# A four-layer cross-attention kernel: its long products issued as four products of 32 output rows, and its value products in blocks of two steps in place of four

## The reference

```python
q = (xn @ wq.T).reshape(B, S, NUM_HEADS, HEAD_DIM)       # x: (8, 100, 128)
k = (kvn @ wk.T).reshape(B, K, NUM_HEADS, HEAD_DIM)      # ctx: (8, 1444, 128)
v = (kvn @ wv.T).reshape(B, K, NUM_HEADS, HEAD_DIM)
scores = jnp.einsum('bshd,bkhd->bhsk', q, k) * scale
attn = jax.nn.softmax(scores, axis=-1)
o = jnp.einsum('bhsk,bkhd->bshd', attn, v).reshape(B, S, D_MODEL)
...
x = _L0_xattn_ref(x, ctx_1024, ...)
x = _L1_xattn_ref(x, ctx_1024, ctx_1024, mask_Bx1xSxS2_bf0, ...)
x = _L2_xattn_ref(x, ctx_1024, ...)      # ff = gelu(att_h @ W1.T + b1) @ W2.T + b2
x = _L3_xattn_ref(x, ctx_1024, ctx_1024, ...)
```

## Time and profile before

| | before |
|---|---|
| median of 3 runs | 1116.84 us (1113.83 to 1118.72) |
| the profiled execution | 1119.34 us, of which the span of its instructions is 1117.6 us |
| PE busy | 1000.5 us, 90% of the span, 9658 products and as many weight loads |
| DVE busy | 818.8 us, 73% |
| ACT busy | 762.0 us, 68% |
| mean granted clock of PE | 0.96 of 2.4 GHz |

### The profile page before, as it was taken

One profiled execution on the slowest core, in us unless ns is written; L12 is line 12 of the kernel. 1 busy time (PEld: TensorE's weight loads), 2 busy tenths in 40 slices (PEclk: granted clock), 3 DMA queues, 4 the chain that ended last, 5 costly groups with the idle time before them and its releaser, 6 DMA issues.

```text
span 1117.6 us, 25480 instructions
## 1 busy us (share of the span) xinstructions
PE 1000.5 (90%) x9658; PEld 554.8 (50%) x9658; DVE 818.8 (73%) x1687; ACT 762.0 (68%) x1692; POOL 414.7 (37%) x411
## 2 busy tenths in 40 slices
PE   0579999999989999999998999999999999998996
PEld 0235555555545555555454555555555545454442
DVE  5697787788767778887887776767677777676851
ACT  1157777876768787878777666666666675757675
POOL 5865545545412341334124142424333342423100
PEclk9979999999999999999999898989898989899999
DMA  8232212321222232223222120202020212111100
GB/s 211 67 94 81 75 52 64 81 72 50 82 63 68 82 105 66 79 81 102 70 81 79 30 80 19 81 18 81 18 83 19 82 36 65 45 55 54 31 4 5
DMA packets 64449, 72.98 MB, mean 65 GB/s; under 512 B 8210, under 2 KB 59994, under 8 KB 64198
## 3 DMA queue, kind: packets, MB, share of 16 engines
q1 hardware_dynamic: 64326, 71.33, 22.7%
HBM read 50.35 MB, written 18.15 MB: 61 GB/s over the span
## 4 chain that ended last, share of the span: by engine, by line
PE 62%; DVE 21%; ACT 8%; issue 5%; POOL 2%; SPq 1%; DMA 0%; POOLq 0%; ACTq 0%; DVEq 0%
PE acc L733 16%; PE ring L674 15%; PE sexp L713 14%; DVE mx L1105 6%; DVE mneg L1111 4%; DVE mx L1103 3%; PE ring L607 3%; PE ring L619 3%; ACT probs L981 2%; PE ring L797 2%; ACT kp L927 2%; PE ring L648 2%; DVE max L1206 1%; SPq L462 1%; ACT sc L1006 1%
## 5 line engine op out<-in xcount | busy, mean ns | idle before, releaser
L1105 DVE TENSOR_TENSOR mx<-ring,mx 120x400 f16<-120x400 f32 (+1 forms) x1056 | 554.5, 567 | 197.0 <-PE ring L674 194.7
L981 ACT ACTIVATE probs<-sexp 120x400 f32<-120x400 f32 (+1 forms) x1152 | 539.6, 513 | 197.5 <-PE sexp L713 192.6
L674 PE MATMUL ring<-qx,krep 96*128 96x400 f16 (+2 forms) x1152 | 398.7, 351 | 43.0 <-ACT kp L927 14.6
L713 PE MATMUL sexp<-qx,krep 97*128 97x400 f16 (+2 forms) x1152 | 396.3, 348 | 8.8 <-ACT probs L981 5.0
L733 PE MATMUL acc<-probs,vx 120*18 120x200 f32 (+1 forms) x4608 | 258.7, 343 | 0.8 <-ACT probs L981 0.7
L713 PEld LDWEIGHTS sexp<-qx,krep 97*128 97x128 f16 (+2 forms) x1152 | 127.0, 111 | 141.1 <-ACT probs L981 79.7
L674 PEld LDWEIGHTS ring<-qx,krep 96*128 96x128 f16 (+2 forms) x1152 | 127.7, 111 | 128.1 <-DVE mx L1105 30.9
L733 PEld LDWEIGHTS acc<-probs,vx 120*18 120x18 f32 (+1 forms) x4608 | 108.0, 98 | 115.7 <-issue 81.8
L481 POOL TENSOR_TENSOR kp<-kf,kp 128x480 f16<-128x480 f32 (+1 forms) x72 | 79.4, 1108 | 204.6 <-ACT kp L927 204.6
L519 POOL TENSOR_TENSOR qx<-qs,headmask 96x400 f16<-96x400 f16 x96 | 80.1, 864 | 54.1 <-PE sexp L713 30.3
L498 POOL TENSOR_TENSOR rstd<-vare,half 100x1 f32<-100x1 f32 x24 | 13.0, 543 | 214.3 <-DVE vare L1122 214.3
(11 more groups left out here) (131 smaller groups left out, 906.4 us busy)
## 6 DMA issues: line engine op xcount, KB each, us to landing
krep<-kept SPq DMA_DIRECT2D x144, 120.0 KB, 2.6
ctf<-in_ctxT SPq DMA_DIRECT2D x16, 722.0 KB
kept<-kp SPq DMA_DIRECT2D x48, 240.0 KB, 2.7
krep<-kept SPq DMA_DIRECT2D x72, 121.0 KB, 3.0
kept<-kp SPq DMA_DIRECT2D x24, 242.0 KB, 2.5
nat<-in_ctx SPq DMA_DIRECT2D x8, 720.0 KB
maskexp<-maskmax SPq DMA_DIRECT2D x8, 281.2 KB, 3.4
anymask<-in_mask SPq DMA_DIRECT2D x1, 1128.1 KB, 7.2
```

What stands on the lines that cost most here:

```text
L674: last = pe.matmul(ps[0:n, 0:QW], krep[0:PARTS, u.par, t, c0:c0 + n], qx[0:PARTS, u.third, t, :, :].rearrange("p f s -> p (f s)"), start=T ...
L713: last = pe.matmul(ps[0:n, 0:QW], krep[:, u.par, t, c0:c0 + n], qx[:, u.third, t, :, :].rearrange("p f s -> p (f s)"), start=True, stop=no ...
L981: act.activation(probs[0:r, j % PR, :], sexp[j % SR][0:r, 0:QW], ACT.Exp).then_inc(sem["probs_ready"], 1)
L1105: op = dve.tensor_tensor(dst, src, dst, ALU.max)
```

## The change

A helper `grouped` issues a product as up to four products of at most 32 output rows each: rows 0 to 31, 32 to 63, 64 to 95 and 96 to the end, each with its own weight load of at most 32 columns. All products of more than 32 output rows go through it except the values' projection (L619), the products of 9 columns (L797), and the transposes of the context, of the mask and of the maxima (L596, L629, L689), which stay as they were. Transposes that go through it (L637, L744, L750, L761, L787, L805) are no longer issued as transposes but as products with the identity; in float32 PE runs each of those as two instructions where it ran one. The number of blocks of values doubles and each has half the products.

```diff
-TOGETHER = 4
+TOGETHER = 2
 VALUES_AT = [j // TOGETHER * TOGETHER + TOGETHER + SR - 1 for j in range(NSTEP)]
...
+        def grouped(run, out, w, x, **flags):
+
+            for g in range(0, out.shape[0], 32):
+                m = min(32, out.shape[0] - g)
+                last = run(out[g:g + m], w[:, g:g + m], x, **flags)
+            return last
...
                 for j, (w, c) in enumerate(((0, 0), (0, 1), (1, 0))):
-                    last = pe.matmul(ps[:, 0:n], wk16[:, w, u.L, :], ct[:, u.par, c, c0:c0 + n], start=(j == 0),
-                                     stop=(j == 2))
+                    last = grouped(pe.matmul, ps[:, 0:n], wk16[:, w, u.L, :], ct[:, u.par, c, c0:c0 + n], start=(j == 0),
+                                   stop=(j == 2), skip_group_check=True)
...
-                last = pe.matmul(ps[0:n, 0:QW], krep[0:PARTS, u.par, t, c0:c0 + n],
-                                 qx[0:PARTS, u.third, t, :, :].rearrange("p f s -> p (f s)"),
-                                 start=True, stop=not masks, skip_group_check=masks)
+                last = grouped(pe.matmul, ps[0:n, 0:QW], krep[0:PARTS, u.par, t, c0:c0 + n],
+                               qx[0:PARTS, u.third, t, :, :].rearrange("p f s -> p (f s)"),
+                               start=True, stop=not masks, skip_group_check=masks)
...
                 for t in range(T):
-                    last = pe.transpose(ps[0:S, 128 * t:128 * t + 128], osb[:, S * t:S * t + S], ident[:, :])
+                    last = grouped(pe.matmul, ps[0:S, 128 * t:128 * t + 128], osb[:, S * t:S * t + S], ident[:, :], start=True,
+                                   stop=True)
...
                 for h in range(HT):
-                    last = pe.transpose(ps[0:S, S * h:S * h + S], sc2[:, HT * t + h, :], ident[0:S, 0:S])
+                    last = grouped(pe.matmul, ps[0:S, S * h:S * h + S], sc2[:, HT * t + h, :], ident[0:S, 0:S], start=True,
+                                   stop=True)
```

More of the change, by code:

```diff
@@ L636, in inputs @@
                 ps = begin("xT", u)
-                pe.transpose(ps[:, 0:S], xcur[:, :], ident[0:S, 0:S]).then_inc(sem["xT_filled"], 1)
+                grouped(pe.matmul, ps[:, 0:S], xcur[:, :], ident[0:S, 0:S], start=True, stop=True).then_inc(sem["xT_filled"], 1)
             def queries(u):
@@ L645, in queries @@
                 if u.L:
-                    pe.matmul(ps[0:PARTS, 0:T * S], bq16[:, u.L, :], which16[:, :], start=True, stop=False, skip_group_check=True)
+                    grouped(pe.matmul, ps[0:PARTS, 0:T * S], bq16[:, u.L, :], which16[:, :], start=True, stop=False,
+                            skip_group_check=True)
                 for t in range(T):
-                    last = pe.matmul(ps[0:PARTS, S * t:S * t + S], wq[:, u.L, t, :], xT[:, :], start=not u.L, stop=True,
-                                     skip_group_check=u.L > 0)
+                    last = grouped(pe.matmul, ps[0:PARTS, S * t:S * t + S], wq[:, u.L, t, :], xT[:, :], start=not u.L,
+                                   stop=True, skip_group_check=u.L > 0)
                 last.then_inc(sem["q_filled"], 1)
             def add_mask(ps, tile, which, c, r):
-                return pe.matmul(ps.rearrange("p (h s) -> p h s", h=HT), masked_by[0:r, which, 0:r],
-                                 tile[0:r, c, :].unsqueeze(1).broadcast_to([r, HT, S]), start=False, stop=True,
-                                 skip_group_check=True)
+                return grouped(pe.matmul, ps.rearrange("p (h s) -> p h s", h=HT), masked_by[0:r, which, 0:r],
+                               tile[0:r, c, :].unsqueeze(1).broadcast_to([r, HT, S]), start=False, stop=True,
+                               skip_group_check=True)
             def columns(c):
@@ L712, in exp_product @@
                 n = columns(c)
-                last = pe.matmul(ps[0:n, 0:QW], krep[:, u.par, t, c0:c0 + n],
-                                 qx[:, u.third, t, :, :].rearrange("p f s -> p (f s)"),
-                                 start=True, stop=not masks, skip_group_check=masks)
+                last = grouped(pe.matmul, ps[0:n, 0:QW], krep[:, u.par, t, c0:c0 + n],
+                               qx[:, u.third, t, :, :].rearrange("p f s -> p (f s)"),
+                               start=True, stop=not masks, skip_group_check=masks)
                 if masks:
@@ L749, in output_back @@
                 ps = begin("OT", u)
-                pe.transpose(ps[:, 0:S], oatt[:, 0, :], ident[0:S, 0:S]).then_inc(sem["oT_filled"], 1)
+                grouped(pe.matmul, ps[:, 0:S], oatt[:, 0, :], ident[0:S, 0:S], start=True, stop=True).then_inc(sem["oT_filled"], 1)
             def project(u):
@@ L754, in project @@
                 ps = begin("wo", u)
-                pe.matmul(ps[0:S, 0:D], oT[:, :], wo[:, u.L, :], start=True, stop=True).then_inc(sem["wo_filled"], 1)
+                grouped(pe.matmul, ps[0:S, 0:D], oT[:, :], wo[:, u.L, :], start=True, stop=True).then_inc(sem["wo_filled"], 1)
             def context_input2(u):
@@ L760, in context_input2 @@
                 ps = begin("cx2", u)
-                pe.transpose(ps[:, 0:S], x2[:, :], ident[0:S, 0:S]).then_inc(sem["cx2_filled"], 1)
+                grouped(pe.matmul, ps[:, 0:S], x2[:, :], ident[0:S, 0:S], start=True, stop=True).then_inc(sem["cx2_filled"], 1)
             def keys_queries_values2(u):
@@ L766, in keys_queries_values2 @@
                 ps = begin("kqv2", u)
-                pe.matmul(ps[:, 0:S], wk[:, 2, :], cx2[:, 0, :], start=True, stop=True)
+                grouped(pe.matmul, ps[:, 0:S], wk[:, 2, :], cx2[:, 0, :], start=True, stop=True)
                 for t in range(T):
                     pe.matmul(ps[32 * t:32 * t + 32, S:2 * S], wq[:, 2, t, 0:32], cx2[:, 1, :], start=True, stop=True)
-                pe.matmul(ps[0:S, 2 * S:2 * S + D], cx2[:, 0, :], wv[:, 2, :], start=True, stop=True
-                          ).then_inc(sem["kqv2_filled"], 1)
+                grouped(pe.matmul, ps[0:S, 2 * S:2 * S + D], cx2[:, 0, :], wv[:, 2, :], start=True, stop=True
+                        ).then_inc(sem["kqv2_filled"], 1)
             def scores2(u, t):
@@ L777, in scores2 @@
                 ps = begin(f"s2{t}", u)
-                pe.matmul(ps[0:S, 0:QW], q2[:, :], kbd2[:, HT * t:HT * t + HT, :].rearrange("p h s -> p (h s)"),
-                          start=True, stop=True).then_inc(sem["s2_filled"], 1)
+                grouped(pe.matmul, ps[0:S, 0:QW], q2[:, :], kbd2[:, HT * t:HT * t + HT, :].rearrange("p h s -> p (h s)"),
+                        start=True, stop=True).then_inc(sem["s2_filled"], 1)
             def transposed2(u, t):
@@ L804, in attention_back2 @@
                 ps = begin("at2", u)
-                pe.transpose(ps[:, 0:S], att2[:, :], ident[0:S, 0:S]).then_inc(sem["at2_filled"], 1)
+                grouped(pe.matmul, ps[:, 0:S], att2[:, :], ident[0:S, 0:S], start=True, stop=True).then_inc(sem["at2_filled"], 1)
             def hidden2(u):
@@ L810, in hidden2 @@
                 for j in range(FF // 128):
-                    last = pe.matmul(ps[:, S * j:S * j + S], w1[:, 128 * j:128 * j + 128], aT2[:, :], start=True, stop=True)
+                    last = grouped(pe.matmul, ps[:, S * j:S * j + S], w1[:, 128 * j:128 * j + 128], aT2[:, :], start=True,
+                                   stop=True)
                 last.then_inc(sem["h2_filled"], 1)
@@ L817, in feed_forward2 @@
                 for j in range(FF // 128):
-                    last = pe.matmul(ps[0:S, 0:D], hT[:, j, :], w2[:, j, :], start=(j == 0), stop=(j == FF // 128 - 1))
+                    last = grouped(pe.matmul, ps[0:S, 0:D], hT[:, j, :], w2[:, j, :], start=(j == 0), stop=(j == FF // 128 - 1),
+                                   skip_group_check=True)
                 last.then_inc(sem["w2_filled"], 1)
```

## The result

The changed kernel takes 1122.8 us (median of 11 runs, 1118.0 to 1128.5), the kernel before 1116.0 us (median of 11, 1112.4 to 1121.3). The ratio is 1.005 with an interval of 1.0029 to 1.007: about half a per cent slower. The forecast was 1107. One of the twelve runs of the first experiment's kernel took 5204.76 us; its ratio leaves that run out. The profiled execution of the changed kernel took 1122.45 us, its span 1120.5.

A forecast was written before the change was run, and what follows sets the result against it. The prediction took PE to set the pace in most places (62% of the chain). Its terms, -48 + 18 + 24 - 5 + 2 = -9 us, gave 1108 by the median, set at 1107 us, with a range of 1085 to 1142.

The forecast's parts named there:

- Nothing is new among the waits: Waits of all engines: exponentials three steps back and engine orders as before, so no new wait was charged.
- Switches taken away, -48: PE's changes between wide and narrow products around value blocks and small products: removing them saves 48 us.
- added, +18: PE's products that stay wide now have a switch on both sides: 97 x 0.19 = +18 us.
- dearer transposes, +24: PE's transposes become float32 identity products of two instructions each, doubling their cost: +24 us on the chain.
- behind a wait, +2: After a PE wait eight instructions follow in place of two, so the last product starts later: +2 us.
- Rounds of four, nothing: PE's score, key and query products: four narrow ones cost the same as one wide; bounds -8 to +15 us.
- The last stage, -5: Last stage, paced by ACT: shorter value blocks remove ACT's idle gaps, 12 x 0.4 = -5 us.
- The clock, a rival with a chance of 0.03: PE's low-clock stretches in layer 2: products replacing transposes hold the clock up, at most 27 us back; chance 0.03.
- DVE takes over: DVE's maxima limit plain steps and swallow PE's gain: 1112 to 1122 for most, 1132 at worst; chance 0.22.
- The waits shrink as well: DVE and ACT get work in even portions, so waits shrink: 16 us more gain, 1091; chance 0.15.
- Feeding: PE's doubled instructions arrive too slowly, deciding from 0.026 us each; 1140 us at 0.028; chance 0.09.

The follow-up runs named there:

- the first experiment: Changed kernel with value products in blocks of four steps again (TOGETHER = 4), narrow products kept: 1118.49 us, ratio 0.9984 to the kernel before.
- third experiment: Changed kernel with a unit's first values at position 6 instead of 4: 1114.26 us, ratio 0.9967 to the kernel before.
- the tenth: Changed kernel with only ACT's two copies of the keys put at one position: ratio 0.9908 to the kernel before, -10.3 us.
- the fifth: Changed kernel with first values at position 6 and ACT's two copies of the keys at one position: 1095.56 us, ratio 0.9803 to the kernel before.
- ninth: Changed kernel with blocks of four and ACT's two copies of the keys at one position: ratio 0.9896 to the kernel before, -11.6 us.
- the sixth: Kernel before with only ACT's two copies of the keys put at one position: ratio 0.9898, -11.4 us.
- second experiment: Kernel before with only blocks of two steps (TOGETHER = 2): ratio 1.0664, +74 us.
- seventh experiment: Changed kernel with first values at position 6 and the values' projection in narrow products too: ratio 1.004 to the kernel before.

## Why the prediction was wrong

The step that failed is "Nothing is new among the waits: a block after every second position has its youngest exponential three steps back, as before, and SP, POOL, ACT and DVE keep their orders". It looked at the exponentials only, and a block waits for more than those. Moving the first block from position 6 to 4 put it ahead of ACT's copy of `acc`, a wait that was put at nothing and cost 9.3 us (third experiment; 11.7 from the tenth to the fifth). The second wait is an old one that blocks of two lengthen: PE's wait for ACT's second copy of the keys, 25.2 us before, 25.6 with narrow products and blocks of four, 30.1 in the changed kernel. What the copies' edit saves says the same by times: 11.4 us on the kernel before, 9.8 with narrow products and blocks of four, 15.9 on the changed kernel and 18.3 on the third experiment's. So some 4 to 9 us of the keys' wait belong to the blocks of two; each saving is known to some 3 us, and a difference of two is no finer than 4. With -9 forecast, +9.3 and the 4.9 us of the wait come to +5, and 5.6 was measured (the medians differ by 6.9). That sums a forecast and measured terms, and the near match is partly luck, since gains that the forecast had left out stand in it too:

| step from one run to the next | us |
|---|---|
| narrow products, blocks of four (first experiment) | -1.8 |
| the keys' copies together (ninth) | -9.8 |
| blocks of two, first values at 6 (fifth) | -10.4 |
| the keys' copies apart again (third) | +18.3 |
| first values at 4 (the changed kernel) | +9.3 |

The last four add up to the 7.4 us that blocks of two cost. The measured time lies inside the range of 1085 to 1142; what was wrong is the direction and the reason. The terms one by one:

- *Switches taken away, -48, and added, +18; dearer transposes, +24; behind a wait, +2.* Their sum, -4, is -1.8 in the first experiment and -0.2 between the ninth and the sixth. The single prices hold: 0.22 us for a block of values among wide products in the second experiment's timeline, 0.88 and 0.70 us a set for the two transposes. L626's set takes 0.81 us where L619's took 0.72, so the way from it back to narrow products is 0.09 us. No run takes the other switches apart.

```profile
494.04 0.88 PE L626 MATMUL ring<-wv,ct 128*120 128x128 f16 x12
494.85 0.35 PE L583 MATMUL sexp<-qx,krep 97*32 97x400 f16 x4
```

- *Rounds of four, nothing.* Right: 0.17 us a round.
- *The last stage, -5.* Right: in the last stage of the changed kernel ACT is without the gaps of 0.39 us of the earlier trace rows; twenty exponentials take 8.32 us, 0.42 each. From ACT's last but one copy of `acc` to its last it is 24.7 us before (1085.83 to 1110.51) and 20.1 after (1092.90 to 1113.03), 4.6 us less.

```profile
1096.09 8.32 ACT L993 ACTIVATE probs<-sexp 121x400 f32<-121x400 f32 x20 [0.43 <-PE sexp L583]
```

- *The clock, a rival with a chance of 0.03.* It was no small thing, and the working that set it low (the transposes end well ahead of the fall) was too quick. In the stretch at layer 2's end the changed kernel has:

```profile
788.00:795.70 7.70, 6.74 (x115) 4.85 (x109) 4.90 (x10) 3.41 (x8) 0.00 (x0) 1.00 0.01 2
795.70:799.10 3.40, 3.40 (x44) 1.66 (x48) 3.00 (x10) 1.01 (x2) 1.51 (x3) 0.50 0.16 35
```

The low stretch is 3.4 us where it was 6.8, at half of 2.4 GHz. Over the span 0.971 in place of 0.960 is 65 us at 1.2 GHz in place of 89, worth up to 12 us. Three pairs that differ only in transposes against identity products all go the same way in their profiled executions: 0.954 against 0.971, 0.960 against 0.970, 0.961 against 0.966. Over all runs the first two pairs stay apart and the third overlaps (0.949 to 0.964 against 0.957 to 0.966). By the Trainium skill (TensorE: Matmul & The Clock Gate, Part 4: PE-mode transpose) a transpose "doesn't count as PE-busy the same way" for the clock, and the first two pairs agree. So the clock may have hidden part of the new waits. That the products alone hold it up does not hold for every kernel here: the first and the third experiment have the same products and mean clocks of 0.961 and 0.963 over their runs, hardly above the kernel before (0.961), and the fifth has stretches of 6.8 us again. What else moves the clock was not told apart.
- *DVE takes over.* Did not happen: its share of the chain fell, and PE's waits for `mx` grew by 2.6 us over all lines.
- *The waits shrink as well.* Half right, and hidden: blocks of two are worth 10 us once neither wait on ACT is in their way, 4.6 of them in the last stage, but with both in place only the opposite is seen.
- *Feeding.* Not in the changed kernel, whose `issue` waits are 4.2 us in all; in the seventh experiment, with 13% more instructions, it seems so. The prediction miscounted here: a plain pair of steps has 24 products and as many loads, 48 and not 40, so in 1.03 us feeding decides from 0.021 us an instruction on and not from 0.026. The changed kernel runs at that pace (48 in 1.02 us).

What stays open: why the shorter blocks lengthen the wait for the keys' copy (the room that a long block gives ACT is argued), how much the clock hides, and how much of a gain in PE's own time DVE's stretch of a stage of layer 0 swallows.

## What to carry to other kernels

When work is moved to an earlier place in a hand-written order, list everything that it overwrites or waits for, not only its inputs: here the buffer's last reader stood one position too late, and one `max(..., 6)` was worth 9 us. Look also for a wait that is already there before the change: putting ACT's two reads of a slot together was worth 10 to 18 us, more than the change itself, and 11 of them were to be had in the kernel before. When a helper takes over the products of many lines, add up the old lines before comparing a wait with the new one. And price a larger number of instructions not only by how fast they run but by whether the queue that brings them keeps up.

## What the runs showed of the hardware

- Four products of 32 output rows and 400 float16 columns take 0.17 us a round, like one of 128 rows; going from wide products to a narrow block and back costs 0.20 to 0.22 us in all (the timelines before and of the second experiment).
- The instruction queue's packets are 79 before and 163 in the changed kernel, for 19316 and 40724 products and loads: some 250 apiece. At 14 ns a pair, 125 pairs are 1.8 us of work (an estimate from these numbers). In the seventh experiment PE stood up to 3.4 us without a wait shown; in the three stalls that were followed it went on at most 2.4 to 2.9 us after a packet began. That packets arrive too slowly fits and is not shown by itself, and the other 11 of the 14 stalls in its view of the waits were not looked at. The page of the seventh experiment's kernel has

```profile
q8 instruction: 184, 3.01, 1.1%
```

- A set of four float32 transposes of 128 columns takes 0.44 us, and 0.88 us as products with an identity (0.35 and 0.70 us with 100 columns). Replacing 24 sets of the first kind and 32 of the second in the kernel before cost 16.8 us for 22 us of work, while the granted clock rose from 0.960 to 0.970; that the clock gave back the difference fits and is not shown.
